# First loads, one product, eight squares and one addition moved in a cross-attention and FFN kernel

## The chip, the core and the metric

The kernel runs on one core of one Trainium2 chip. The core has five engines, each with an instruction queue of its own that is worked off in order: TensorE (PE, matrix products; PEld is its weight load), VectorE (DVE), ScalarE (ACT), GpSimd (POOL) and SyncE (SP, which here only issues DMAs). Engines wait for each other through semaphores. The metric is the device time of one launch in microseconds (us), the median of several runs; lower is better.

## The reference

There are 128 sequences of 64 rows with 128 features. `_prob` is a shifted tanh divided by its row sum. Cut to what is computed:

```python
def xattn(q, k, v, ...):                      # q = layernorm(x), k = v = ctx
    q_prob, k_prob = _prob(q), _prob(k)
    log_ratio = jnp.log(q_prob) - jnp.log(k_prob)
    sid = jnp.einsum('bnd,bmd->bnm', q_prob - k_prob, log_ratio)
    attn = jax.nn.softmax(-sid / D ** 0.5, axis=-1)
    f_diff = (v - attn @ v) @ W_diff.T + b_diff + q
    h = _layernorm(f_diff, ln_g, ln_b)
    mlp = gelu(h @ W1.T + b1) @ W2.T + b2     # 128 -> 512 -> 128
    return _layernorm(mlp + f_diff, ln_g, ln_b)

x = x + xattn(layernorm(x), ctx, ctx, ...)
x = x + fp8_linear(layernorm(x), weight) + bias
```

## The kernel before

The 8192 rows are 64 tiles of 128 rows. Four tiles are a chunk (16 chunks); in stages two and three the last chunk is cut into two halves, which makes 17 pieces (NA = NP = 17), numbered from 0. Every stage is a software pipeline: `run_steps` calls a step function per engine, in which `at(lag)` is the piece that entered `lag` steps ago. The order on each engine is the order in which the step function is written.

**Stage one** (`phase1`, to 62.9 us). Per chunk SP loads ctx and x into two buffers each: the load of ctx chunk k waits until ACT has taken the tanh of chunk k-2 (`tanh_k`) and PE has turned it, that of x until DVE has the variance of chunk k-2 (`x_var`). PE transposes ctx (L1058) and multiplies it by W_diff (L1067), then adds the row b_diff with a selection matmul (L1076). ACT takes tanh of ctx (L556), copies the transposed ctx (L561) and the product (L567), and takes tanh of normalised x (L572). DVE computes the statistics of x (L835 to L798), normalises x into F (L867) and adds the product to F (L840). POOL raises the variance to the power -0.5 (L376) and adds the row ln_b to X (`add_to_x`, L368) for the final residual. The rows b_diff and ln_b come in by two DMAs (L546, L547) that ACT's queue issues; DVE centres b_diff and splits it in two parts (L750 to L764) ahead of its first chunk.

**Stage two** (`phase2`, to about 122 us). Per piece: ACT takes Ln (L617), Exp of the scores (L627), copies two transposed operands out of PSUM (L642 and L644, called dT and lT), and makes half of the k parts of the difference (L607). DVE finishes the difference (L904) and the log ratio (L916), and adds the attention product to F (L939). POOL does the k parts of two tiles (L389) and the whole of one tile (L395, L409, L400, L414). PE transposes difference and log ratio (L1166, L1172), forms the scores (L1154) and the attention product (L1139). In the last steps the MLP of the first two pieces is prepared: ACT squares F with a sum (L599, `squares`, four tiles each), takes Ln and Exp of the variance (L653, L656), DVE scales F into h (L878, `take_h`), PE turns h (L1099, `turn_h`), ACT and DVE split it in a high part (L588, `upper_half`) and a low part (L883, `lower_half`), and PE begins the first matmuls (L1109 to L1111, `mlp1`). Before the first gelu (L594) ACT loads another function table (L630).

**Stage three** (`phase3`). The MLP, the second norm, both residuals and the quantised linear layer, with the same kind of pipeline. Variances of pieces 2 on come from `squares` on ACT and `norm_power` on POOL (L507, L509), in pairs of pieces. POOL also issues DMAs that add bias rows to F (L441, L497), and between the stages quantises the weight of the last layer (L457 to L469).

The functions that the change touches, with the lines of the profile:

## Time and profile before

| | us |
|---|---|
| median of 3 runs | 255.77 (255.61 to 256.09) |
| the profiled execution's own time | 255.62 |
| its span, first to last instruction | 253.7 |
| TensorE's mean granted clock | 0.958 of full speed |

| engine | busy us | share of the span | instructions |
|---|---|---|---|
| PE | 210.8 | 83% | 1777 |
| DVE | 221.2 | 87% | 842 |
| ACT | 216.9 | 86% | 781 |
| POOL | 190.6 | 75% | 255 |

A busy share is an average over three stages with different limits, so each stage is read by itself: which engine never waits there, and who is waited for. Instructions of one engine overlap a little in the record (the next one starts some 0.1 us before the last one's end is written), so spacings are taken from start to start. The profiled execution's time is 1.92 us more than its span, and 0.15 us under the median.

### The profile page before, as it was taken

The page shows a single profiled execution, that of the slowest core. Times are in us where ns is not written, and L with a number is a line of the kernel's source. Part 1 is how long each engine was busy: PE and PEld are TensorE (multiplying, and loading weights), DVE is VectorE, ACT ScalarE, POOL GpSimd, SP SyncE. Part 2 cuts the span into 40 slices and gives each one's busy share as a digit, 9 for nine tenths or more (in the row PEclk, how much of TensorE's full clock was granted, in tenths as well). Part 3 has the DMA queues.
Part 4 walks back from the last instruction along what each step waited for, and adds up shares of the span by engine and source line. Part 5 has one row for each costly group of instructions (what it writes and reads, how often), then busy time and mean ns, then how long its engine had stood idle before and what let it go on. Part 6 is the DMA issues. An engine that isn't in the chain of part 4 may idle for free.

```text
span 253.7 us, 6046 instructions
## 1 busy us (share of the span) xinstructions
PE 210.8 (83%) x1777; PEld 181.4 (71%) x1777; DVE 221.2 (87%) x842; ACT 216.9 (86%) x781; POOL 190.6 (75%) x255
## 2 busy tenths in 40 slices
PE   2686685987499888877899999999999999998721
PEld 1666463876386666656699999988998999887610
DVE  1899999998899999999525889999999999999983
ACT  4599999998999999979997889998888777876673
...
GB/s 136 191 191 199 162 153 164 162 115 16 3 3 0 3 3 1 3 1 3 44 25 93 18 98 145 98 148 111 145 128 120 131 144 119 127 129 115 97 43 124
DMA packets 50817, 23.52 MB, mean 93 GB/s; under 512 B 9313, under 2 KB 50657, under 8 KB 50785
## 3 DMA queue, kind: packets, MB, share of 16 engines
...
q10 hardware_dynamic: 432, 0.20, 0.3%
q14 instruction: 19, 0.15, 0.2%
...
## 4 chain that ended last, share of the span: by engine, by line
POOL 30%; DVE 24%; issue 11%; PE 6%; ACT 4%; DVEq 0%; POOLq 0%; ACTq 0%
POOL F L441 6%; POOL xrstd L483 5%; POOL orstd L476 4%; POOL F L497 4%; DVE q_c L904 3%; DVE F L939 3%; PE bank L1118 3%; POOL q_c L389 3%; DVE LN_c L916 3%; DVE F L962 3%; DVE xstat L973 2%; DVE LN_c L982 2%; POOL LN_c L409 2%; DVE F L967 2%; POOL E_c L395 2%
## 5 line engine op out<-in xcount | busy, mean ns | idle before, releaser
L1118 PEld LDWEIGHTS bank<-W2T,TQK 128*128 128x128 f32 x512 | 62.9, 191 | 4.6 <-ACT TQK L594 1.3
L1118 PE MATMUL bank<-W2T,TQK 128*128 128x128 f32 x512 | 64.5, 277 | 1.1 <-ACT TQK L594 1.1
L594 ACT ACTIVATE TQK<-bank,b1c 128x512 f32<-128x512 f32 (+1 forms) x68 | 42.9, 662 | 5.6 <-PE bank L1111 5.0
L483 POOL TENSOR_TENSOR xrstd<-xvar,pow_c 128x4 f32<-128x4 f32 (+1 forms) x17 | 18.6, 1093 | 20.1 <-DVE xvar L798 20.1
L376 POOL TENSOR_TENSOR xrstd<-xvar,pow_c 128x4 f32<-128x4 f32 x16 | 16.8, 1052 | 22.0 <-DVE xvar L798 22.0
L1109 PE MATMUL bank<-hTh,W1h 128*128 128x512 f32 (+1 forms) x68 | 30.0, 442 | 0.8 <-DVE hTl L883 0.8
L441 POOL DMA_DIRECT2D F<-rows x17 | 26.0, 1529 | 5.8 <-DVE E_c L878 5.8
L1110 PE MATMUL bank<-hTl,W1h 128*128 128x512 f32 (+1 forms) x68 | 26.0, 382 | 0.0
L1111 PE MATMUL bank<-hTh,W1l 128*128 128x512 f32 (+1 forms) x68 | 25.8, 380 | 0.0
L1067 PE MATMUL bank<-WdT,vT_c 128*128 128x128 f32 x128 | 21.3, 318 | 3.4 <-ACT vT_c L561 2.6
L1067 PEld LDWEIGHTS bank<-WdT,vT_c 128*128 128x128 f32 x128 | 18.8, 226 | 5.7 <-ACT vT_c L561 5.7
L1058 PE MATMUL bank<-ident,LN_c 128*128 128x128 f32 x64 | 12.6, 330 | 11.0 <-DMA LN_c<-in_ctx_dram 10.9
L556 ACT ACTIVATE TQK<-LN_c 128x128 f32<-128x128 f32 x64 | 19.4, 335 | 1.9 <-DMA LN_c<-in_ctx_dram 1.9
L497 POOL DMA_DIRECT2D F<-rows x14 | 18.6, 1326 | 3.2 <-issue 2.7
L368 POOL TENSOR_TENSOR X<-X,rows 128x512 f32<-128x512 f32 x16 | 20.4, 1272 | 0.4 <-DVE F L867 0.3
L572 ACT ACTIVATE TQK<-F 128x128 f32<-128x128 f32 x64 | 19.6, 347 | 0.7 <-DVE F L867 0.7
L678 ACT ACTIVATE TQK<-F 128x128 f32<-128x128 f32 x64 | 19.0, 313 | 0.7 <-DVE F L957 0.7
L904 DVE SCALAR_TENSOR_TENSOR q_c<-TQK,GAINQ,q_c 128x128 f32<-128x128 f32 x49 | 19.6, 450 | 0.0
L1139 PE MATMUL bank<-PV,E_c 64*64 64x129 f32 x256 | 18.3, 281 | 1.4 <-ACT E_c L627 1.4
L711 ACT ACTIVATE LN_c<-LN_c 128x512 bf16<-128x512 fp8e4 x13 | 8.2, 631 | 13.1 <-DVE LN_c L982 13.1
L1058 PEld LDWEIGHTS bank<-ident,LN_c 128*128 128x128 f32 x64 | 8.8, 168 | 14.5 <-DMA LN_c<-in_ctx_dram 14.2
L599 ACT ACTIVATE TQK<-F 128x128 f32<-128x128 f32 x64 | 19.0, 311 | 0.0
...
## 6 DMA issues: line engine op xcount, KB each, us to landing
...
```

What stands on the lines that cost most here:

```text
L368: pool.tensor_tensor(tiles(chunk(X, k)), tiles(chunk(X, k)), over_tiles(b_r, k.g), ALU.add).then_inc(xb_ready, 1)
L441: pool.dma_start(tiles(chunk(F, k)), over_tiles(b2_r, k.g), accum_op=ALU.add).then_inc(b2_added[k.n % 3], 16)
L483: pool.tensor_tensor(buf(xrstd, x1, G), buf(xvar, x1, G), pow_c[:, 0:x1.g], ALU.pow).then_inc(x1_rstd, 1)
L497: pool.dma_start(tiles(chunk(F, x1)), over_tiles(bf_r, x1.g), accum_op=ALU.add).then_inc(bf_added[x1.n % 3], 16)
L594: act.activation(hid(m, j), m1_bank(m, j), ACT.Gelu, bias=b1c[:, j:j + 1]).then_inc(gelu_ready, 1)
L904: last = dve.scalar_tensor_tensor(out=tile(diff_c, k, i), in0=all_tile(TQ, k, i), scalar=per_tile(GAINQ, k, i), in1=tile(diff_c, k, i), op ...
L1058: last = pe.transpose(VT_B[k.buf][:, i * D:(i + 1) * D], tile(ctx_c, k, i), ident[:, :])
L1067: last = pe.matmul(P_B[k.n % 3][:, i * D:(i + 1) * D], tile(vT_c, k, i), WdT[:, :], start=(i == 0), stop=False, skip_group_check=True)
L1109: pe.matmul(ps, w_hi, buf(hTh, m), start=True, stop=False)
L1110: pe.matmul(ps, w_hi, buf(hTl, m), start=False, stop=False)
L1111: pe.matmul(ps, w_lo, buf(hTh, m), start=False, stop=True).then_inc(m1_ps, 1)
L1118: last = pe.matmul(M2_B[m.buf][:, i * D:(i + 1) * D], hid(m, j)[:, i * D:(i + 1) * D], W2T[:, j * D:(j + 1) * D], start=(j == 0 and i == 0 ...
```

## The change

1. SP issues the loads of ctx and x for chunks 0 and 1, then the two rows b_diff and ln_b, then goes on. ACT issues only W_diff.
2. DVE centres and splits b_diff after the normalisation of chunk 0, and no longer ahead of the first statistics.
3. PE multiplies chunk 0 by W_diff before it transposes chunk 1, and ACT copies this product between the tanh of chunk 1 and the copy of the transposed chunk 1.
4. The squares of pieces 0 and 1 are no longer two runs of four in steps 15 and 16 of stage two. Each of the steps 7 to 14 has one, between the copies dT and lT. Ln and Exp follow for both pieces together in step 15.
5. `take_h`, `turn_h`, `upper_half` and `lower_half` of piece 0 each come one step earlier.
6. POOL's addition of ln_b to the last chunk of X leaves step 15 of stage two and comes after `norm_power` of piece 3.

```diff
@@ -91,2 +91,3 @@
     EARLY = 2
+    SQUARES_AT = 6
     NORM_CUTS = (0, 4, 8, NC)
@@ -319,3 +320,7 @@
 
-            for k in chunks[0:5]:
+            for k in chunks[0:2]:
+                load(k)
+            sp.dma_start(bd_r, b_diff.unsqueeze(0).broadcast_to([P, D])).then_inc(bd_in, 16)
+            sp.dma_start(b_r, ln_b.unsqueeze(0).broadcast_to([P, D])).then_inc(br_in, 16)
+            for k in chunks[2:5]:
                 load(k)
@@ -432,4 +437,2 @@
                         log_ratio(k, G - 1)
-                if is_piece(k, NA - 2):
-                    add_to_x(chunks[NC - 1])
 
@@ -527,2 +530,3 @@
             norm_power(pieces[3])
+            add_to_x(chunks[NC - 1])
             run_steps(pieces, 1, phase3)
@@ -545,4 +549,2 @@
             act.dma_start(Wd_raw, W_diff).then_inc(wd_in, 16)
-            act.dma_start(bd_r, b_diff.unsqueeze(0).broadcast_to([P, D])).then_inc(bd_in, 16)
-            act.dma_start(b_r, ln_b.unsqueeze(0).broadcast_to([P, D])).then_inc(br_in, 16)
             act.wait_ge(wd_ps, 1)
@@ -550,2 +552,8 @@
 
+            def keep_product(k):
+                act.wait_ge(P_ps, k.n + 1)
+                if is_piece(k, 0):
+                    act.wait_ge(consts, CONSTS)
+                act.activation(pv_chunk(k), tiles(P_B[k.n % 3][:, 0:k.g * D]), ACT.Copy).then_inc(P_sb, 1)
+
             def phase1(at):
@@ -558,2 +566,4 @@
                     last.then_inc(tanh_k, 1)
+                    if is_piece(k, 1):
+                        keep_product(chunks[0])
                     act.wait_ge(vT_ps, k.n + 1)
@@ -562,7 +572,4 @@
                 k = at(1)
-                if k.live:
-                    act.wait_ge(P_ps, k.n + 1)
-                    if is_piece(k, 0):
-                        act.wait_ge(consts, CONSTS)
-                    act.activation(pv_chunk(k), tiles(P_B[k.n % 3][:, 0:k.g * D]), ACT.Copy).then_inc(P_sb, 1)
+                if k.live and k.n > 0:
+                    keep_product(k)
                 k = at(2)
@@ -595,2 +602,6 @@
 
+            def square(k, i):
+                return act.activation(all_tile(TK, k, i), all_tile(F, k, i), ACT.Square,
+                                      scale=float(D) ** -0.5, accum_out=per_tile(VARF, k, i))
+
             def squares(k):
@@ -598,4 +609,3 @@
                 for i in range(k.g):
-                    last = act.activation(all_tile(TK, k, i), all_tile(F, k, i), ACT.Square,
-                                          scale=float(D) ** -0.5, accum_out=per_tile(VARF, k, i))
+                    last = square(k, i)
                 last.then_inc(fvar_ready, 1)
@@ -642,2 +652,9 @@
                     act.activation(buf(dT_c, k), D_B[:, 0:k.g * D], ACT.Copy).then_inc(dT_sb, 1)
+                    nth = k.n - SQUARES_AT
+                    if 0 <= nth < EARLY * G:
+                        first = pieces[nth // G]
+                        act.wait_ge(f_half, (first.at + first.g) // 2)
+                        last = square(first, nth % G)
+                        if nth % G == G - 1:
+                            last.then_inc(fvar_ready, 1)
                     act.wait_ge(lT_ps, k.n + 1)
@@ -647,13 +664,11 @@
                     kparts(k)
-                k = at(0)
-                if k.n >= NA - 2 and k.live:
-                    first = pieces[k.n - (NA - 2)]
-                    squares(first)
-                    act.wait_ge(fvar_ready, first.n + 1)
-                    act.activation(of_tiles(VARF, first), of_tiles(VARF, first), ACT.Ln,
+                if is_piece(at(1), SQUARES_AT + EARLY * G):
+                    act.wait_ge(fvar_ready, EARLY)
+                    act.activation(VARF[:, 0:EARLY * G], VARF[:, 0:EARLY * G], ACT.Ln,
                                    bias=eps_c[:, 0:1]).then_inc(fln_ready, 1)
-                    act.wait_ge(fln_ready, first.n + 1)
-                    act.activation(of_tiles(RSTDF, first), of_tiles(VARF, first), ACT.Exp,
-                                   scale=-0.5).then_inc(frstd, 1)
-                if is_piece(at(2), NA - 2):
+                    act.wait_ge(fln_ready, 1)
+                    for first in pieces[0:EARLY]:
+                        act.activation(of_tiles(RSTDF, first), of_tiles(VARF, first), ACT.Exp,
+                                       scale=-0.5).then_inc(frstd, 1)
+                if is_piece(at(2), NA - 3):
                     upper_half(pieces[0])
@@ -771,6 +786,2 @@
             dve.tensor_copy(sel[:, :], sel_raw).then_inc(sel_ready, 1)
-            dve.wait_ge(bd_in, 16)
-            centre_row(bd_r, 0).then_inc(bd_ready, 1)
-            dve.wait_ge(bd_ready, 1)
-            split_row(bd_r, bd_hl[:, :], 0).then_inc(bd_hl_ready, 1)
 
@@ -869,2 +880,7 @@
                     last.then_inc(q_ready, 1)
+                if is_piece(q, 0):
+                    dve.wait_ge(bd_in, 16)
+                    centre_row(bd_r, 0).then_inc(bd_ready, 1)
+                    dve.wait_ge(bd_ready, 1)
+                    split_row(bd_r, bd_hl[:, :], 0).then_inc(bd_hl_ready, 1)
 
@@ -926,8 +942,7 @@
                     centre_row(b2_r, 2).then_inc(rows_ready, 1)
-                if is_piece(k, NA - 1):
+                if is_piece(k, NA - 2):
                     dve.wait_ge(frstd, 1)
+                    dve.wait_ge(diff_pool, NC - 1)
                     take_h(pieces[0])
                 k = at(2)
-                if is_piece(k, NA - 2):
-                    lower_half(pieces[0])
                 if k.live:
@@ -943,2 +958,4 @@
                             last.then_inc(f_half, 1)
+                if is_piece(k, NA - 3):
+                    lower_half(pieces[0])
                 if is_piece(k, NA - 2):
@@ -959,2 +976,4 @@
             def residual(x1):
+                if is_piece(x1, NC - 1):
+                    dve.wait_ge(xb_ready, NC)
                 dve.wait_ge(orstd_ready, x1.n + 1)
@@ -1021,3 +1040,3 @@
 
-            dve.wait_ge(xb_ready, NC)
+            dve.wait_ge(xb_ready, NC - 1)
             run_steps(pieces, 1, phase3)
@@ -1046,2 +1065,10 @@
 
+            def products(k):
+                pe.wait_ge(vT_sb, k.n + 1)
+                wait(pe, pq_ready, k.n - 2)
+                for i in range(k.g):
+                    last = pe.matmul(P_B[k.n % 3][:, i * D:(i + 1) * D], tile(vT_c, k, i), WdT[:, :],
+                                     start=(i == 0), stop=False, skip_group_check=True)
+                last.then_inc(P_ps, 1)
+
             def phase1(at):
@@ -1052,2 +1079,5 @@
                     keep_busy(10)
+                if is_piece(at(1), 0):
+                    pe.wait_ge(wd_sb, 1)
+                    products(at(1))
                 k = at(0)
@@ -1059,12 +1089,4 @@
                     last.then_inc(vT_ps, 1)
-                k = at(1)
-                if k.live:
-                    if is_piece(k, 0):
-                        pe.wait_ge(wd_sb, 1)
-                    pe.wait_ge(vT_sb, k.n + 1)
-                    wait(pe, pq_ready, k.n - 2)
-                    for i in range(k.g):
-                        last = pe.matmul(P_B[k.n % 3][:, i * D:(i + 1) * D], tile(vT_c, k, i), WdT[:, :],
-                                         start=(i == 0), stop=False, skip_group_check=True)
-                    last.then_inc(P_ps, 1)
+                if at(1).live and at(1).n > 0:
+                    products(at(1))
                 k = at(2)
@@ -1125,3 +1147,3 @@
                 k = at(2)
-                if is_piece(k, NA - 2):
+                if is_piece(k, NA - 3):
                     turn_h(pieces[0])
```

In the following rows the line numbers of the kernel after the change differ from those of before; the operands tell which is which.

DVE, from its first statistics to the statistics of chunk 2. Before, with the five instructions on b_diff (`rows`, `row_mean`, `bd_hl`) in front:

```order
L750 TENSOR_REDUCE row_mean<-rows 128x1
L752 TENSOR_SCALAR row_mean<-row_mean 128x1
L754 TENSOR_SCALAR rows<-rows,row_mean 128x128
L761 CAST bd_hl<-rows 128x128
L764 TENSOR_TENSOR bd_hl<-rows,bd_hl 64x128
L835 BN_STATS xstat<-X 128x6 x4
```

After, the end of the normalisation of chunk 0 (F) and what stands behind it:

```order
L878 TENSOR_SCALAR F<-X,xmv,xrstd 128x128 x4
L765 TENSOR_REDUCE row_mean<-rows 128x1
L767 TENSOR_SCALAR row_mean<-row_mean 128x1
L769 TENSOR_SCALAR rows<-rows,row_mean 128x128
L776 CAST bd_hl<-rows 128x128
L779 TENSOR_TENSOR bd_hl<-rows,bd_hl 64x128
L846 BN_STATS xstat<-X 128x6 x4
```

The five instructions have moved from in front of everything to between chunk 0's F and chunk 2's statistics.

ACT, steps 15 and 16 of stage two, from the copy dT (`vT_c<-bank`) of piece 14 to the table load. Before (NRATIO holds the variances, HALFK their inverse roots):

```order
L642 ACTIVATE vT_c<-bank 128x512
L644 ACTIVATE lT_c<-bank 128x512
L607 ACTIVATE q_c<-TQK,SHIFT,GAINK 128x128
L599 ACTIVATE TQK,NRATIO<-F 128x128 x4
L653 ACTIVATE NRATIO<-NRATIO,eps_c 128x4
L656 ACTIVATE HALFK<-NRATIO 128x4
L617 ACTIVATE LN_c<-TQK,half_c 128x2x256
L627 ACTIVATE E_c<-bank 128x256
L642 ACTIVATE vT_c<-bank 128x256
L644 ACTIVATE lT_c<-bank 128x256
L599 ACTIVATE TQK,NRATIO<-F 128x128 x4
```

After:

```order
L652 ACTIVATE vT_c<-bank 128x512
L661 ACTIVATE lT_c<-bank 128x512
L617 ACTIVATE q_c<-TQK,SHIFT,GAINK 128x128
L667 ACTIVATE NRATIO<-NRATIO,eps_c 128x8
L671 ACTIVATE HALFK<-NRATIO 128x4 x2
L627 ACTIVATE LN_c<-TQK,half_c 128x2x256
L637 ACTIVATE E_c<-bank 128x256
L652 ACTIVATE vT_c<-bank 128x256
L661 ACTIVATE lT_c<-bank 128x256
L595 ACTIVATE hTh<-bank 128x512
```

Both runs of four squares are gone from here, and the upper half of piece 0 follows in the same step.

POOL, from the weight's last product to the first bias DMAs of stage three. Before:

```order
L469 TENSOR_TENSOR NORM<-NORM,RNORM 128x128
L507 TENSOR_TENSOR NRATIO<-NRATIO,eps_c 128x8
L509 TENSOR_TENSOR HALFK<-NRATIO,pow_c 128x8
L441 DMA F<-rows 128x4x128
L507 TENSOR_TENSOR NRATIO<-NRATIO,eps_c 128x8
```

After:

```order
L472 TENSOR_TENSOR NORM<-NORM,RNORM 128x128
L510 TENSOR_TENSOR NRATIO<-NRATIO,eps_c 128x8
L512 TENSOR_TENSOR HALFK<-NRATIO,pow_c 128x8
L373 TENSOR_TENSOR X<-X,rows 128x512
L444 DMA F<-rows 128x4x128
```

The addition to X now stands directly behind the power for which DVE's `take_h` of piece 2 waits.

## Rows read from the trace of the kernel before

**Rows 1.** Windows: stretch, length, busy us (and instructions) of each engine, clock, DMA.
```profile
20.00:40.00 20.00, 14.23 (x93) 12.05 (x94) 19.30 (x96) 20.00 (x111) 13.64 (x12) 0.91 0.59 169
...
80.00:100.00 20.00, 17.77 (x244) 13.89 (x244) 20.00 (x76) 19.50 (x39) 19.41 (x37) 1.00 0.01 2
...
160.00:200.00 40.00, 40.00 (x291) 36.47 (x290) 37.73 (x129) 36.17 (x132) 32.67 (x33) 1.00 0.91 129
```
**Rows 2.** Timeline, first 13 us: start, duration, engine, line, count, [idle before, releaser].
```profile
5.89 0.29 DVE L750 TENSOR_REDUCE row_mean<-rows 128x1 f32<-128x128 f32 x1 [4.17 <-DMA rows<-in_L_xattn_b_diff_dram]
...
6.98 0.29 DVE L764 TENSOR_TENSOR bd_hl<-rows,bd_hl 64x128 fp32r<-64x128 f32 x1
7.65 0.87 DVE L835 BATCH_NORM_STATS2 xstat<-X 128x6 f32<-128x128 f32 x4 [0.38 <-DMA X<-in_x_dram]
...
8.57 0.31 ACT L556 ACTIVATE TQK<-LN_c 128x128 f32<-128x128 f32 x1 [1.89 <-DMA LN_c<-in_ctx_dram]
...
11.45 0.60 ACT L567 ACTIVATE PV<-bank 128x512 f32<-128x512 f32 x1 [1.11 <-PE bank L1067]
...
12.19 1.26 POOL L368 TENSOR_TENSOR X<-X,rows 128x512 f32<-128x512 f32 x1
...
12.36 0.87 DVE L835 BATCH_NORM_STATS2 xstat<-X 128x6 f32<-128x128 f32 x4 [0.33 <-DMA X<-in_x_dram]
```
**Rows 3.** Timeline of DVE, 21 to 29 us.
```profile
21.68 0.87 DVE L835 BATCH_NORM_STATS2 xstat<-X 128x6 f32<-128x128 f32 x4 [0.17 <-DMA X<-in_x_dram]
...
28.02 0.87 DVE L835 BATCH_NORM_STATS2 xstat<-X 128x6 f32<-128x128 f32 x4
28.99 0.69 DVE L840 TENSOR_TENSOR F<-bank,F 128x512 f32<-128x512 f32 x1
```
**Rows 4.** Timeline, end of stage one.
```profile
59.40 1.27 POOL L368 TENSOR_TENSOR X<-X,rows 128x512 f32<-128x512 f32 x1
59.90 0.86 DVE L867 TENSOR_SCALAR F<-X,xmv,xrstd 128x128 f32<-128x128 f32 x1
...
61.56 0.31 ACT L572 ACTIVATE TQK<-F 128x128 f32<-128x128 f32 x1 [0.65 <-DVE F L867]
```
**Rows 5.** Timeline, one step in the middle of stage two.
```profile
95.04 1.14 ACT L617 ACTIVATE LN_c<-TQK,half_c 128x1024 f32<-128x1024 f32 x1
...
96.34 0.59 ACT L642 ACTIVATE vT_c<-bank 128x512 f32<-128x512 f32 x1
96.82 0.60 POOL L409 TENSOR_SCALAR LN_c<-LN_c,LRATIO 128x128 f32<-128x128 f32 x1
...
97.02 0.60 ACT L644 ACTIVATE lT_c<-bank 128x512 f32<-128x512 f32 x1
```
**Rows 6.** Timeline, last steps of stage two.
```profile
111.78 1.29 POOL L368 TENSOR_TENSOR X<-X,rows 128x512 f32<-128x512 f32 x1
...
111.87 1.35 DVE L916 SCALAR_TENSOR_TENSOR LN_c<-LN_c,LRATIO 128x128 f32<-128x128 f32 x1
...
115.11 0.30 ACT L599 ACTIVATE TQK<-F 128x128 f32<-128x128 f32 x1
...
115.40 0.29 ACT L599 ACTIVATE TQK<-F 128x128 f32<-128x128 f32 x1
...
117.88 1.10 PE L1139 MATMUL bank<-PV,E_c 64*64 64x129 f32 x16 [1.45 <-ACT E_c L627]
...
121.70 1.28 ACT L630 ACT_TABLE_LOAD   x1
...
122.16 0.47 PE L1109 MATMUL bank<-hTh,W1h 128*128 128x512 f32 x1 [0.80 <-DVE hTl L883]
```
**Rows 7.** Timeline, start of stage three.
```profile
130.08 1.38 POOL L441 DMA_DIRECT2D F<-rows  x1
...
130.20 0.69 DVE L878 TENSOR_TENSOR E_c<-F,HALFK 128x512 f32<-128x512 f32 x1 [3.14 <-POOL HALFK L509]
...
131.21 0.60 PE L1099 MATMUL bank<-ident,E_c 128*128 128x128 f32 x4
```

## The prediction

> **What bounds the kernel now.** I read the windows first, because the shares over the whole span mix three stages. In stage one ACT is busy all the time and DVE 19.30 of 20 us; in stage two DVE is busy all the time, with ACT (19.50) and POOL (19.41) close behind; in stage three PE is busy 40.00 of 40 us [rows 1]. So three things count: when DVE finishes stage one, how long the steps of stage two are, and when PE can begin the MLP. Then I read the timeline at both borders. At the end of stage one ACT is the one that waits: its last tanh stands 0.65 us idle for DVE's F [rows 4]. So DVE, not ACT, ends stage one, although ACT has the fuller row. From 122.16 us PE runs without a pause that matters; what it waits for there (0.80 us) is the lower half of piece 0 [rows 6]. A shift of that point reaches the end, unless PE is stopped later.
>
> **The first loads.** The two rows on ACT's queue are 64 KB each and share the 16 DMA engines with the first four chunk loads. DVE's first statistics begin at 7.65, behind 0.38 us of waiting for x, and ACT's second tanh at 8.57, behind 1.89 us of waiting for ctx [rows 2]. Up to 7.65 about 1.1 MB have come in, of which the rows are 0.13; in proportion they cost (0.13/1.1) x (7.65 - 2) = 0.6 us. The engines aren't full in this stretch, so less can come of it: I take 0.4, from 0.2 to 0.6. SP issues the rows two places ahead of the load of ctx chunk 2, which waits for the first tanh in any case, so they delay nothing. ACT gains more than the 0.4: the product of chunk 0 is no longer behind the transposes of chunk 1, so most of the 1.11 us ahead of the copy at 11.45 goes too [rows 2]. ACT will be about 1.1 us early. I book none of it, since ACT waits for DVE at the end of the stage anyway.
>
> **The five DVE instructions on b_diff.** They run from 5.89 to 7.27, 1.38 us [rows 2]. Before, all but nothing of this cost time, as x landed only later. Now they stand between F of chunk 0 and the statistics of chunk 2, on the engine that ends the stage. DVE waited 0.33 us until 12.36 for x, so it was free at 12.03, or 11.95 with the usual overlap; with 0.4 us gained that is 11.55, and with some 1.3 us added start to start the statistics of chunk 2 begin at 12.9 instead of 12.36: +0.5. DVE then loses waits that it has now. The wait for x of 0.17 at 21.68 goes, with 0.1 in front of it, and three times (as at 28.99, where L840 starts 0.10 after the end of the statistics in front) L840 waits 0.1 to 0.2 us for ACT's tanh, which now comes earlier [rows 3]. That is 0.7 in all. So alone, moving them costs 0.5 - 0.7 = -0.2 us: nothing.
> But they get a neighbour. POOL starts the addition to X (L368, 1.26 us) 0.15 us after F of chunk 0 [rows 2], that is at 11.8 to 13.05, just beside them. At the end of the stage a DVE instruction of the same form as the third of them (tensor_scalar, 128x128) that begins while L368 runs takes 0.86 us and ends 0.09 after L368 does [rows 4]; three of four such instructions in the same group take about 0.34. By this row the third instruction, due at 12.1, ends at 13.2 instead of 12.3, and the fourth and fifth follow: +0.85. Stage one then ends 0.65 us later than before. Range: -0.2 (no collision) to +0.8. I take 0.65, since the form is the same.
>
> **The squares in the steps of stage two.** A square with its sum takes 0.29 us from start to start (115.11 to 115.40) [rows 6]. In a step ACT's copy dT begins at 96.34 and the next, lT, at 97.02; dT lasts 0.59, and its neighbours of that size follow each other after 0.5. So 0.1 to 0.18 us per step is spare and the square adds 0.1 to 0.2 to each of eight steps: ACT falls behind by 0.8 (up to 1.6) at the end. What hides this is distance: Ln begun at 95.04 ends at 96.18, and POOL uses it at 96.82, 0.64 us later [rows 5]; DVE uses it only some 2.4 us later, and the k parts 2.1 us later. Until the seventh square ACT is 0.7 behind. I book 0.1 us; the range is 0 to 0.9. Where the cover is gone, POOL and soon DVE move by what is over.
>
> **The last steps of stage two.** Three terms, not to be added, since they lie beside each other; I followed the chain with the durations of the trace.
> First, L368 at 111.78 goes. Beside it one L916 took 1.35 us instead of about 0.3 [rows 6]: -1.0 on DVE, and PE's transposes of log ratio, ACT's lT and all behind them follow.
> Second, ACT has no squares (4 x 0.29 = 1.2 us, with Ln and Exp 1.7) ahead of Ln of piece 16 and Exp of piece 14. PE waited 1.45 us for that Exp, until 117.88 [rows 6]. Now: lT of piece 14 at 113.3, the shared Ln and two Exps to 114.8, Ln of piece 16 to 115.4, Exp to 115.8, and PE at 116.1. That is -1.8.
> Third, the chain of h. `take_h` of piece 0 runs at 114.7 to 115.4, so the upper half is ready at 116.9. The lower half then waits only for its turn on DVE, behind F of piece 14: 118.95 to 119.6. PE begins the MLP at 119.65 instead of 122.16: -2.5. On ACT the last Exp follows at 119.25, the table load (1.28 us, before at 121.70 [rows 6]) at 119.5, and gelu can begin at 120.8, 2.2 us earlier than the load ends now (122.98). So PE is 2.5 and ACT 2.2 us early, less what stages one and two give away.
> POOL reaches the weight's quantisation some 3 us earlier and has it done before it is wanted.
>
> **The moved addition on POOL.** Only about one microsecond of POOL's time is shifted here, and POOL waits again later. The neighbour is the question again. Before, behind the power (L509) POOL issues a DMA at 130.08, and DVE, released by the same power, starts `take_h` of piece 2 at 130.20; PE turns it at 131.21 [rows 7], 0.32 us after it ends at 130.89. Now L368 stands in the DMA's place and begins 0.1 us ahead of `take_h`, which reads two SBUF operands as L916 did. L916, begun 0.09 after L368, ended 0.15 after it [rows 6]. Its 128 columns fit into that; `take_h` has 512, about 0.55 us of work, so it would end near 130.08 + 1.27 + 0.55 = 131.9, 1.0 late. PE has 0.3 us to spare. At this point the gain is then 2.2 + 0.3 - 1.0 = 1.5 us instead of 2.5. If `take_h` wins, POOL waits and the gain is 2.5. I take 1.5: POOL was first by about as much in the row.
> The Trainium skill ("SBUF — State Buffer", section Who interferes with whom) says that a DVE instruction with two SBUF inputs and a GpSimd one that reads SBUF exclude each other, and whichever starts first holds the ports for all of its instruction. By this rule both collisions happen, unless DVE is first at `take_h`; the rows on L916 and L867 agree with it.
>
> **Sum**, against the profiled execution: +0.65 (stage one) + 0.1 (steps) - 1.5 (border of stage three) = -0.75 us. It measured 255.62, 0.15 under the median of the runs shown; set against that median of 255.77 I get 255.0 us.
>
> **The rivals.**
> A. One collision only. Without that on b_diff: -0.2 + 0.1 - 1.5 = -1.6; without that on `take_h`: 0.65 + 0.1 - 2.5 = -1.75. About 254.1. For it speaks that 0.1 us decides who is first; against it that POOL came first in both rows.
> B. No collision: -0.2 + 0.1 - 2.5 = -2.6, 253.2. It needs both 0.1 us to fall the other way.
> C. ACT becomes the bound of stage two, and the kernel gets slower. If a lone square costs ACT its 0.30 and the read of its sum 0.19 one after the other instead of 0.29, each step is over by 0.3 to 0.4, 8 steps by 2.4 to 3.1; less the 0.64 of cover that leaves about 2.1, of which I take 2.0 as late at the border. Then +0.65 + 2.0 - 1.5 = +1.15, 256.9. It decides from 0.24 us over per step ((0.75 + 0.64 + 0.5)/8). Against it: four squares in a row, and a copy behind such a tanh, all follow after 0.29.
> D. The change doesn't do what it says: the gain is kept by something else at the border, for instance rows b_diff that ACT's earlier tanh doesn't need and a `lower_half` that still waits. Then only stage one counts, and the time is 255.6 to 256.2.
>
> **How the numbers follow.** Forecast 0.47, A 0.30, B 0.09, C 0.07, D 0.07. The forecast's own terms give 255.0 within 0.5. The range takes in the forecast, A and the better part of D, and leaves out C and most of B: 253.5 to 255.9. A measurement of this kernel can tell about 0.2%, 0.5 us, from no change. Faster by more than that, under 255.26: two thirds of the forecast (0.32), A and B, 0.71. Within it: the rest of the forecast and most of D, 0.20. Slower: C and a rest of D, 0.09.
>
> **What the profile would show.** Right: the last tanh of stage one waits longer than 0.65 us for DVE; the third of the b_diff instructions lasts near 1 us; the steps of stage two stay at 3.25 us; in step 14 no L916 over 0.5 us; PE's first MLP matmul 1.7 to 2.0 us earlier than 122.16; `take_h` of piece 2 lasts over 1.2 us, and PE stops behind it. Wrong: steps with squares longer than 3.3 us, POOL waiting for Ln in them, a first MLP matmul at 122 or later, or a stage one that ends earlier than before.

## The result, and the profile after

| | before | after |
|---|---|---|
| median of 4 runs each, side by side | 255.69 (255.22 to 256.09) | 253.16 (252.62 to 253.33) |
| the profiled execution's own time | 255.62 | 252.62 |
| its span | 253.7 | 250.7 |

The ratio of the runs is 0.9892, 95% interval 0.9871 to 0.9912: 2.5 us faster by the medians, 2.8 by the ratio, and faster by more than the forecast, whose range ended at 253.5. A second set of runs of the changed kernel gave the same ratio (0.9892, 0.9872 to 0.9911). Two executions of the experiments below were in a slower state (403.61 and 501.79 us) and count in no ratio.

The rows of the changed kernel that answer to those of before, group by group. Line numbers have moved: L846 is DVE's statistics, L878 its normalisation, L373 POOL's addition to X, L604 ACT's square, L1131 the first MLP matmul.

Windows, as [rows 1] (columns: stretch, length, busy us and instructions of PE, PEld, DVE, ACT, POOL, clock, DMA share, GB/s):

```profile
20.00:40.00 20.00, 15.05 (x100) 12.40 (x100) 19.60 (x98) 20.00 (x111) 13.77 (x12) 0.93 0.59 164
80.00:100.00 20.00, 17.93 (x252) 13.90 (x248) 20.00 (x74) 20.00 (x49) 19.41 (x39) 1.00 0.01 2
160.00:200.00 40.00, 40.00 (x291) 36.34 (x291) 37.95 (x125) 34.89 (x123) 32.40 (x35) 1.00 0.88 129
```

In stage two ACT has become as full as DVE (20.00 of 20 us, 19.50 before); the rest stands as it was.

Timeline of the first 13 us, as [rows 2]:

```profile
5.21 0.87 DVE L846 BATCH_NORM_STATS2 xstat<-X 128x6 f32<-128x128 f32 x4 [3.48 <-DMA X<-in_x_dram]
...
6.22 0.30 ACT L564 ACTIVATE TQK<-LN_c 128x128 f32<-128x128 f32 x1
...
8.55 0.60 ACT L557 ACTIVATE PV<-bank 128x512 f32<-128x512 f32 x1 [1.06 <-PE bank L1070]
...
9.81 1.27 POOL L373 TENSOR_TENSOR X<-X,rows 128x512 f32<-128x512 f32 x1
...
10.08 1.08 DVE L769 TENSOR_SCALAR rows<-rows,row_mean 128x128 f32<-128x128 f32 x1
...
11.79 0.87 DVE L846 BATCH_NORM_STATS2 xstat<-X 128x6 f32<-128x128 f32 x4
```

Here lies the surprise. The first statistics begin 2.44 us earlier (5.21, not 7.65), ACT's second tanh 2.35 us earlier (6.22, not 8.57). The forecast had 0.4. Then DVE does the five instructions on b_diff, of which the third (L769) takes 1.08 us beside POOL's addition, as forecast, and the statistics of chunk 2 begin at 11.79, still 0.57 earlier than before.

End of stage one, as [rows 4]:

```profile
58.60 1.69 DVE L878 TENSOR_SCALAR F<-X,xmv,xrstd 128x128 f32<-128x128 f32 x4
...
60.33 0.31 ACT L579 ACTIVATE TQK<-F 128x128 f32<-128x128 f32 x1 [0.89 <-DVE F L878]
```

The last tanh waits 0.89 us for DVE (0.65 before) and begins 1.23 us earlier (61.56 before); forecast was 0.65 later.

One step of stage two, as [rows 5]:

```profile
94.11 1.18 ACT L627 ACTIVATE LN_c<-TQK,half_c 128x1024 f32<-128x1024 f32 x1
...
95.41 0.63 ACT L652 ACTIVATE vT_c<-bank 128x512 f32<-128x512 f32 x1
...
95.89 0.35 ACT L604 ACTIVATE TQK<-F 128x128 f32<-128x128 f32 x1
...
96.18 0.64 ACT L661 ACTIVATE lT_c<-bank 128x512 f32<-128x512 f32 x1
...
97.43 1.19 ACT L627 ACTIVATE LN_c<-TQK,half_c 128x1024 f32<-128x1024 f32 x1
```

The square (L604) stands between the copies dT and lT; they start 0.77 us apart instead of 0.68, and the step lasts 3.32 us instead of 3.25.

The last steps, as [rows 6], and the start of stage three, as [rows 7]:

```profile
110.43 0.92 DVE L932 SCALAR_TENSOR_TENSOR LN_c<-LN_c,LRATIO 128x128 f32<-128x128 f32 x3
...
114.88 1.10 PE L1161 MATMUL bank<-PV,E_c 64*64 64x129 f32 x16
...
118.40 1.28 ACT L640 ACT_TABLE_LOAD   x1
...
118.65 0.47 PE L1131 MATMUL bank<-hTh,W1h 128*128 128x512 f32 x1 [0.59 <-DVE hTl L899]
```
```profile
124.66 0.20 POOL L510 TENSOR_TENSOR NRATIO<-NRATIO,eps_c 128x8 f32<-128x8 f32 x1 [1.71 <-ACT TQK L604]
...
126.59 1.29 POOL L373 TENSOR_TENSOR X<-X,rows 128x512 f32<-128x512 f32 x1
126.70 1.73 DVE L894 TENSOR_TENSOR E_c<-F,HALFK 128x512 f32<-128x512 f32 x1 [3.14 <-POOL HALFK L512]
...
128.49 0.66 PE L1121 MATMUL bank<-ident,E_c 128*128 128x128 f32 x4 [0.62 <-DVE E_c L894]
```

DVE's three log ratios of that step take 0.92 us together, and none meets the addition. PE's attention product behind the freed Exp begins at 114.88 instead of 117.88: 3.00 earlier, of which 1.23 come from stage one and 1.77 from here (forecast 1.8). The MLP begins at 118.65 (122.16 before). POOL's addition at 126.59 is 0.11 us ahead of the scaling of piece 2, which takes 1.73 us instead of 0.69, and PE waits 0.62 us for it.

Measured from the last tanh of stage one, so that the stages come apart (single executions, start to start):

| | before | after | difference | forecast |
|---|---|---|---|---|
| last tanh of stage one begins | 61.56 | 60.33 | -1.23 | +0.65 |
| from there to the first MLP matmul | 60.60 | 58.32 | -2.28 | -2.4 |
| from there to PE's turn of piece 2 | 69.65 | 68.16 | -1.49 | -1.4 |
| from that turn to the end of the span | 122.49 | 122.21 | -0.28 | 0 |

So the second half of the forecast held in this execution almost to the tenth (some of that is luck, as the spread of these stretches shows further down), and the first half failed. The experiments ask what made the first loads so much faster, and what each part of the change is worth.

### The profile page after: what moved, and what is told of

It is laid out like the page before. It is cut to its first block, busy times and chain, and to the rows that moved or that the text cites. A ratio compares the mean times of both kernels' runs of the same rounds, so it can differ in the third digit from the quotient of the medians.

```text
span 250.7 us, 6047 instructions
## 1 busy us (share of the span) xinstructions
PE 212.1 (85%) x1777; PEld 181.2 (72%) x1777; DVE 221.9 (89%) x842; ACT 216.3 (86%) x780; POOL 191.1 (76%) x255
## 4 chain that ended last, share of the span: by engine, by line
POOL 29%; ACT 14%; DVE 14%; issue 13%; PE 5%; DVEq 0%; ACTq 0%; POOLq 0%
POOL F L444 8%; POOL xrstd L486 7%; POOL orstd L479 5%; POOL F L500 5%; ACT LN_c L627 3%; ACT q_c L617 3%; DVE LN_c L932 2%; DVE q_c L920 2%; POOL HALFK L512 2%; DVE F L954 2%; ACT lT_c L661 1%; ACT E_c L637 1%; PE bank L1140 1%; ACT vT_c L652 1%; DVE F L981 1%
## 5 line engine op out<-in xcount | busy, mean ns | idle before, releaser
L1131 PE MATMUL bank<-hTh,W1h 128*128 128x512 f32 (+1 forms) x68 | 30.0, 442 | 0.6 <-DVE hTl L899 0.6
L373 POOL TENSOR_TENSOR X<-X,rows 128x512 f32<-128x512 f32 x16 | 20.3, 1271 | 0.2 <-DVE F L878 0.2
L579 ACT ACTIVATE TQK<-F 128x128 f32<-128x128 f32 x64 | 19.7, 354 | 0.9 <-DVE F L878 0.9
L693 ACT ACTIVATE TQK<-F 128x128 f32<-128x128 f32 x64 | 19.0, 313 | 1.0 <-DVE F L974 1.0
L604 ACT ACTIVATE TQK<-F 128x128 f32<-128x128 f32 x64 | 19.5, 319 | 0.0
L627 ACT ACTIVATE LN_c<-TQK,half_c 128x1024 f32<-128x1024 f32 (+1 forms) x17 | 19.0, 1118 | 0.0
L726 ACT ACTIVATE LN_c<-LN_c 128x512 bf16<-128x512 fp8e4 x13 | 8.2, 632 | 12.1 <-DVE LN_c L1001 12.1
L479 POOL TENSOR_TENSOR orstd<-ovar,pow_c 128x4 f32<-128x4 f32 (+1 forms) x17 | 17.3, 1016 | 1.3
L1001 DVE TENSOR_SCALAR LN_c<-F,xmv,xrstd 128x128 fp8e4<-128x128 f32 x56 | 15.6, 343 | 2.9 <-POOL xrstd L486 2.7
```

The lines of the kernel that those rows point to most:

```text
L479: pool.tensor_tensor(buf(orstd, k, G), buf(ovar, k, G), pow_c[:, 0:k.g], ALU.pow).then_inc(orstd_ready, 1)
L627: act.activation(ln_both(k), tanh_both(k), ACT.Ln, bias=half_c[:, 0:1], scale=TANH_GAIN).then_inc(ln_ready, 1)
L1131: pe.matmul(ps, w_hi, buf(hTh, m), start=True, stop=False)
```

## The experiments

All ratios are to the kernel before, run on the same chip beside the kernel in question; where two of them are compared, their difference times 255.7 us is the price, good to 0.6 to 0.8 us by the intervals. The two kernels compared did not always run on the same chip, which the ratios can only take out as far as it touches both alike. "Stage one" stands for DVE's and ACT's new order and the rows' new place together.

### What stretched the first loads

**Theory B**: a load that copies one row of HBM to 128 partitions reads the same 512 B 128 times, is slow for its 64 KB, and beside the chunk loads on a second queue holds them up. **Rivals**: any transfer on a second queue does that (Q); only the bytes count (M); or the gain at the start came from the new order (O).

**Rows back on ACT's queue, all else changed.**

```diff
-            sp.dma_start(bd_r, b_diff.unsqueeze(0).broadcast_to([P, D])).then_inc(bd_in, 16)
-            sp.dma_start(b_r, ln_b.unsqueeze(0).broadcast_to([P, D])).then_inc(br_in, 16)
...
             act.dma_start(Wd_raw, W_diff).then_inc(wd_in, 16)
+            act.dma_start(bd_r, b_diff.unsqueeze(0).broadcast_to([P, D])).then_inc(bd_in, 16)
+            act.dma_start(b_r, ln_b.unsqueeze(0).broadcast_to([P, D])).then_inc(br_in, 16)
```

> The changed kernel with one thing put back: the two row loads (b_diff, ln_b) are issued by ACT's queue right behind W_diff, as before the change. Everything else stays changed. Theory S (the row loads stretched the loads of the first chunks from beside them, and taking them away gave about 2.2 us of the gain): x of chunk 0 lands as late as before, DVE's first statistics at about 7.6 us and not 5.2, chunk 2's statistics about 12.6 to 13.0, time 255.0 to 255.6. Rival O (the gain at the start came from the new order of work on PE, ACT and DVE, and the early landing only filled it): first statistics at 7.6 but chunk 2's at 11.8 to 12.1, time 253.2 to 253.8.

Measured 255.28 us, ratio 0.9983 (0.9965 to 1.0001). Its timeline:

```profile
7.47 0.87 DVE L846 BATCH_NORM_STATS2 xstat<-X 128x6 f32<-128x128 f32 x4 [5.75 <-DMA X<-in_x_dram]
```
```profile
62.46 0.31 ACT L579 ACTIVATE TQK<-F 128x128 f32<-128x128 f32 x1 [0.89 <-DVE F L878]
```

x of chunk 0 is late again by 2.26 us (7.47 against 5.21), and stage one ends 2.13 us later than in the changed kernel (62.46 against 60.33). Nearly all of the shift at the start reaches the end of the stage. By the ratios the loads' place is worth 2.3 us: O has fallen. My figure for the statistics of chunk 2 (12.6 to 13.0) missed: they begin at 14.02, 2.23 us later than in the changed kernel.

**Two more loads on ACT's queue: dense, and broadcast.** Both kernels are the changed one with one pair of loads added, into free space of `lT_c`.

```diff
             act.dma_start(Wd_raw, W_diff).then_inc(wd_in, 16)
+            act.dma_start(lT_c[:, C + 0*D:C + 1*D], W_diff).then_inc(extra_in, 16)
+            act.dma_start(lT_c[:, C + 1*D:C + 2*D], W_diff).then_inc(extra_in, 16)
```
```diff
             act.dma_start(Wd_raw, W_diff).then_inc(wd_in, 16)
+            act.dma_start(lT_c[:, C + 0*D:C + 1*D], b_diff.unsqueeze(0).broadcast_to([P, D])).then_inc(extra_in, 16)
+            act.dma_start(lT_c[:, C + 1*D:C + 2*D], ln_b.unsqueeze(0).broadcast_to([P, D])).then_inc(extra_in, 16)
```

> The changed kernel, and ACT issues two more loads of 64 KB behind its own W_diff, each of the whole matrix W_diff into free space (128 rows of 512 B that lie behind one another in HBM). Theory B (what stretches the first chunk loads is that a row load reads the same 512 B 128 times): these do not, x of chunk 0 lands 0.2 to 0.5 us later than in the changed kernel (their bytes, 0.13 MB at some 300 GB/s, are 0.4 us), time 253.2 to 253.7. Rival Q (any transfer of a second queue takes its share beside SP's): first statistics near 7.6 us and time 255.0 to 255.6, as with the row loads on ACT.

> The changed kernel, and ACT issues two more row loads (b_diff and ln_b again, broadcast to 128 partitions, 64 KB each) behind W_diff, into free space; nobody waits for them before stage two. Theories B and Q both say first statistics at 7.3 to 7.9 us and time 255.0 to 255.9; the bytes alone (theory M) say 5.6 us and 253.2 to 253.7.

Measured: dense 252.98 us, ratio 0.9897 (0.9869 to 0.9924), no different from the changed kernel; broadcast 256.27 us, ratio 1.0019 (1.0002 to 1.0036), 3.2 us more than the changed kernel by the ratios and 3.1 more than the dense pair. The same queue, size and place; only the source differs. The dense pair cost even less than theory B had booked for its bytes: x of chunk 0 came 0.10 us later (5.31 against 5.21) where 0.2 to 0.5 were expected, and the time is 0.2 under the expected range. The DMA view of the first 9 us of the one with dense loads (columns: what, issuing engine, count, size, median us from issue to landing):

```profile
X<-in_x_dram SPq DMA_DIRECT2D x3, 256.0 KB, 4.0
lT_c<-in_L_xattn_W_diff_dram ACTq DMA_DIRECT2D x2, 64.0 KB, 3.5
```

and of the one with broadcast loads:

```profile
LN_c<-in_ctx_dram SPq DMA_DIRECT2D x3, 256.0 KB, 5.4
X<-in_x_dram SPq DMA_DIRECT2D x3, 256.0 KB, 5.6
...
lT_c<-in_L_xattn_b_diff_dram ACTq DMA_DIRECT2D x1, 64.0 KB, 4.4
lT_c<-in_L_xattn_ln_b_dram ACTq DMA_DIRECT2D x1, 64.0 KB, 6.1
rows<-in_L_xattn_b_diff_dram SPq DMA_DIRECT2D x1, 64.0 KB, 7.7
```

Two dense loads land 3.5 us after their issue and leave x at 4.0 (3.9 in the changed kernel); two broadcast ones take 4.4 and 6.1, and x takes 5.6. The windows of 3 to 6 us (the DMA share is added up from the times of the packets and can come out above 1) say what the DMA engines do meanwhile, with the dense pair and then with the broadcast pair:

```profile
3.00:4.00 1.00, 0.56 (x2) 0.50 (x2) 0.00 (x0) 0.43 (x1) 0.00 (x0) 1.00 1.12 335
4.00:5.00 1.00, 1.00 (x5) 0.72 (x4) 0.00 (x0) 0.75 (x5) 0.00 (x0) 1.00 1.15 310
5.00:6.00 1.00, 0.32 (x2) 0.00 (x0) 0.69 (x4) 1.00 (x7) 0.00 (x0) 1.00 1.20 296
```
```profile
3.00:4.00 1.00, 0.45 (x2) 0.48 (x2) 0.00 (x0) 0.45 (x1) 0.00 (x0) 1.00 0.78 225
4.00:5.00 1.00, 1.00 (x6) 0.73 (x5) 0.00 (x0) 0.65 (x4) 0.00 (x0) 1.00 0.51 146
5.00:6.00 1.00, 0.29 (x2) 0.00 (x0) 0.00 (x0) 1.00 (x7) 0.00 (x0) 1.00 0.89 258
```

With dense loads beside them the chunks come in at some 300 GB/s, with broadcast loads at 225, 146 and 258, and the DMA engines show as busy for only 0.51 of the time at the lowest point, though three loads of 256 KB are still to come in (ctx of chunk 0 landed at 4.1 us). The kernel before and the changed one show the same pair of pictures (before first):

```profile
3.00:4.00 1.00, 0.04 (x1) 0.07 (x1) 0.00 (x0) 0.43 (x1) 0.00 (x0) 1.00 0.68 196
4.00:5.00 1.00, 1.00 (x4) 0.83 (x5) 0.00 (x0) 0.24 (x2) 0.00 (x0) 1.00 0.52 136
```
```profile
3.00:4.00 1.00, 0.40 (x2) 0.43 (x2) 0.00 (x0) 0.00 (x0) 0.00 (x0) 1.00 1.12 336
4.00:5.00 1.00, 0.99 (x5) 0.69 (x5) 0.00 (x0) 0.60 (x4) 0.00 (x0) 1.00 1.03 281
```

Theory B stands, Q and M have fallen. The Trainium skill ("DMA: Bandwidth & Descriptors", section Rules for kernel authors) says that loads issued by different engines run on the same 16 DMA engines and interleave, so that a second queue gives no bandwidth; the dense pair agrees (335, 310 and 296 GB/s in the three windows, 336, 281 and 289 without it), and the page says nothing of what a broadcast source costs. Two of my numbers for the broadcast pair missed: x came at 6.83 and not at 7.3 to 7.9, and the time was 0.4 above my range. The second x chunk was delayed still more (its statistics began at 9.93; 6.94 in the changed kernel, 9.19 with the two rows back on ACT's queue). These 0.74 us over the kernel with the rows back are there again at the last tanh (63.20 against 62.46). SP's own queue was held too: its issue of the row b_diff took 1.72 us, 0.58 in the changed kernel. Why such a load stalls the others while the engines show as half idle isn't settled.

**The rows with SP, but the old order.** The kernel before with the loads' move alone.

```diff
-            act.dma_start(bd_r, b_diff.unsqueeze(0).broadcast_to([P, D])).then_inc(bd_in, 16)
-            act.dma_start(b_r, ln_b.unsqueeze(0).broadcast_to([P, D])).then_inc(br_in, 16)
...
-            for k in chunks[0:5]:
+            for k in chunks[0:2]:
+                load(k)
+            sp.dma_start(bd_r, b_diff.unsqueeze(0).broadcast_to([P, D])).then_inc(bd_in, 16)
+            sp.dma_start(b_r, ln_b.unsqueeze(0).broadcast_to([P, D])).then_inc(br_in, 16)
+            for k in chunks[2:5]:
                 load(k)
```

> The kernel before with one thing changed: SP and not ACT issues the two row loads, behind the loads of chunks 0 and 1. DVE still centres b_diff ahead of its first statistics. Theory S: x of chunk 0 has landed by 5.2 us, but DVE now waits for the row until about 8.1 us and its five instructions end at about 9.5, so its first statistics begin at about 9.6 (7.65 before): the loads alone cost 1 to 2 us, 256.7 to 257.7. If the time is under 255.7, DVE's place behind the row was no loss and the loads' move is worth its gain alone.

Measured 256.59 us, ratio 1.0028 (1.0007 to 1.0050): 0.7 us slower than before, just under what I expected. DVE waits for b_diff until 7.66 us (I had 8.1) and begins its statistics at 9.07. So each half of the change in stage one, by itself, makes the kernel slower: the loads alone +0.7, and the new order alone +1.5 (next section). Together they gain 0.8. The loads bring x in early, and the new order lets DVE use it.

### What each half of the change is worth

**The border alone**: stage one and its loads as before, everything else as changed.

```diff
-            sp.dma_start(bd_r, b_diff.unsqueeze(0).broadcast_to([P, D])).then_inc(bd_in, 16)
-            sp.dma_start(b_r, ln_b.unsqueeze(0).broadcast_to([P, D])).then_inc(br_in, 16)
...
+            act.dma_start(bd_r, b_diff.unsqueeze(0).broadcast_to([P, D])).then_inc(bd_in, 16)
+            act.dma_start(b_r, ln_b.unsqueeze(0).broadcast_to([P, D])).then_inc(br_in, 16)
...
+            dve.wait_ge(bd_in, 16)
+            centre_row(bd_r, 0).then_inc(bd_ready, 1)
+            dve.wait_ge(bd_ready, 1)
+            split_row(bd_r, bd_hl[:, :], 0).then_inc(bd_hl_ready, 1)
...
-                if is_piece(q, 0):
-                    dve.wait_ge(bd_in, 16)
-                    centre_row(bd_r, 0).then_inc(bd_ready, 1)
-                    dve.wait_ge(bd_ready, 1)
-                    split_row(bd_r, bd_hl[:, :], 0).then_inc(bd_hl_ready, 1)
```

(and the product of chunk 0 back in its old place on PE and ACT).

> The kernel with the second half of the change alone: squares of pieces 0 and 1 in the steps, the MLP work of piece 0 one step earlier, POOL's last addition in stage three. Loads, b_diff on DVE and the first product are as before. Theory of the prediction (the border is worth 1.5 us, the steps with squares cost 0.1): last tanh of stage one at 61.6 us as before, first MLP matmul near 119.8 (122.16 before), piece 2's turn near 129.8 (131.2), time 253.9 to 254.5. Rival E (the steps with squares cost nothing and the border's whole 2.4 us stay): 253.0 to 253.5. Rival N (the gain of the whole change is all at the start): 255.3 to 255.9.

Measured 253.89 us, ratio 0.9923 (0.9907 to 0.9938).

```profile
61.17 0.31 ACT L577 ACTIVATE TQK<-F 128x128 f32<-128x128 f32 x1 [0.77 <-DVE F L880]
```
```profile
119.49 0.47 PE L1127 MATMUL bank<-hTh,W1h 128*128 128x512 f32 x1 [0.58 <-DVE hTl L896]
...
127.54 1.72 DVE L891 TENSOR_TENSOR E_c<-F,HALFK 128x512 f32<-128x512 f32 x1 [3.14 <-POOL HALFK L510]
```

From the last tanh to the MLP it is 58.32 us, the very figure of the changed kernel (by luck, given the spread below), and the scaling of piece 2 takes its 1.72 us. The time lies at the fast edge of the theory's range: -2.0 us by the ratio, where the forecast had -1.4 for steps and border together. The trace accounts for -1.5 up to the turn of piece 2 and -0.3 behind it. It also shows how far a single execution can be trusted: stage one is the same code as before and ends 0.39 us earlier.

The parts, from the ratios:

| part | from, to | price in us | forecast |
|---|---|---|---|
| squares, steps and border | before, border alone | -2.0 | -1.4 |
| new order of stage one, rows on ACT's queue | border alone, rows back on ACT's queue | +1.5 | +1.05 |
| rows to SP's queue | rows back on ACT's queue, changed kernel | -2.3 | -0.4 |
| all | before, changed kernel | -2.8 | -0.75 |

**The last addition back in stage two.**

```diff
+                if is_piece(k, NA - 2):
+                    add_to_x(chunks[NC - 1])
...
             norm_power(pieces[3])
-            add_to_x(chunks[NC - 1])
```

> The changed kernel with one thing put back: POOL adds ln_b to the last chunk of X in step 15 of stage two again, and not behind the power of piece 3. Theory: the log ratio or another DVE instruction of the last steps meets it and loses 0.6 to 0.8 us there, while the scaling of piece 2 takes 0.69 us and not 1.73, so piece 2's turn comes at about the same time: within 0.3 us of the changed kernel, 252.8 to 253.4. Rival W (the addition's old place was worth the whole border): 254.0 to 254.7.

Measured 252.94 us, ratio 0.9880 (0.9861 to 0.9899): no different from the changed kernel, as the theory says. The scaling of piece 2 takes 0.69 us again, but the MLP begins 59.47 us after the last tanh instead of 58.32, and the turn of piece 2 comes at 68.52 us instead of 68.16. So moving the addition gained nothing that can be told in sum, which fits what the theory says: what it frees in stage two it takes back in stage three. In stage two the addition (113.12, 1.27 us) meets two of DVE's differences (L921), which take 0.86 us together and 0.60 in the changed kernel: 0.26 us, where I had 0.6 to 0.8. The rest of the 1.15 us can't be put down to it, since that stretch varies by a microsecond by itself (more on this below).

### The two collisions

**The addition one place earlier**, in POOL's 1.71 us of waiting ahead of 124.66.

```diff
-            norm_power(pieces[3])
             add_to_x(chunks[NC - 1])
+            norm_power(pieces[3])
```

> The changed kernel with POOL's last addition one place earlier: ahead of the power of piece 3 and not behind it, into the 1.7 us in which POOL waits for ACT's squares. Theory P (the scaling of piece 2 takes 1.73 us because it meets the addition): it takes 0.69 us, piece 2's turn comes 0.7 to 1.0 us earlier, and the time falls by 0.4 to 0.9 us to 252.2 to 252.7. Rival: stage three is bound by PE and ACT and the start of piece 2 is made good within it, so that 0 to 0.2 us are left (252.8 to 253.1).

Measured 252.51 us, ratio 0.9870 (0.9850 to 0.9889).

```profile
123.60 1.28 POOL L373 TENSOR_TENSOR X<-X,rows 128x512 f32<-128x512 f32 x1
...
127.39 0.69 DVE L894 TENSOR_TENSOR E_c<-F,HALFK 128x512 f32<-128x512 f32 x1 [3.14 <-POOL HALFK L512]
...
128.40 0.60 PE L1121 MATMUL bank<-ident,E_c 128*128 128x128 f32 x4
```

The collision is gone: the same scaling takes 0.69 us with the addition out of its way, 1.73 beside it. By the ratios that is worth 0.6 us, within what the theory said, though the intervals overlap; the same edit made once more below gives 0.6 again. In this execution the MLP began at 119.34, 0.69 us later than in the changed kernel's, in a stretch that the edit doesn't touch, which hides the gain in the timeline's own times.

**POOL's first addition held back** until b_diff is split.

```diff
                     if is_piece(k, 0):
                         pool.wait_ge(br_in, 16)
+                        pool.wait_ge(bd_hl_ready, 1)
```

> The changed kernel with POOL's first addition to X held until DVE has split b_diff (a wait on POOL). Theory P: DVE's subtraction of the row's mean takes 0.29 us and not 1.08, so the statistics of chunk 2 begin about 0.8 us earlier (11.0 us), unless they meet the addition in turn; 0.5 to 0.8 us of it reach the end of stage one, time 252.2 to 252.7. Rival: the collision only moves to the statistics or the next normalisation and nothing is won: 252.8 to 253.3.

Measured 252.88 us, ratio 0.9889 (0.9867 to 0.9911): nothing won.

```profile
9.98 0.29 DVE L770 TENSOR_SCALAR rows<-rows,row_mean 128x128 f32<-128x128 f32 x1
...
10.89 0.87 DVE L847 BATCH_NORM_STATS2 xstat<-X 128x6 f32<-128x128 f32 x4
...
11.00 1.27 POOL L373 TENSOR_TENSOR X<-X,rows 128x512 f32<-128x512 f32 x1 [1.33 <-DVE bd_hl L780]
...
11.87 0.42 DVE L795 TENSOR_TENSOR xmv<-xstat 128x8 f32<-128x8 f32 x1
```

The subtraction of the mean takes 0.29 us and not 1.08, and the statistics of chunk 2 begin 0.90 us earlier than in the changed kernel. But now the addition meets the small instructions behind the statistics (L795 takes 0.42 us, 0.17 in the changed kernel), and of the 0.90 us 0.65 are left at the statistics of chunk 3 (13.85 against 14.50) and 0.29 at the last tanh (60.04 against 60.33). The rival was right: the collision only moved.

### A version that beats both

The selection matmul uses only partitions 0 and 64 of b_diff (its selection matrix is zero elsewhere). So two loads of 512 B can take the place of 128 reads, early enough for DVE to do its five instructions while x is still on its way.

```diff
             act.dma_start(Wd_raw, W_diff).then_inc(wd_in, 16)
+            act.wait_ge(bd_zero, 1)
+            act.dma_start(bd_r[0:1, :], b_diff.unsqueeze(0)).then_inc(bd_in, 16)
+            act.dma_start(bd_r[S:S + 1, :], b_diff.unsqueeze(0)).then_inc(bd_in, 16)
...
-            sp.dma_start(bd_r, b_diff.unsqueeze(0).broadcast_to([P, D])).then_inc(bd_in, 16)
...
+            dve.memset(bd_r, 0.0).then_inc(bd_zero, 1)
...
+            dve.wait_ge(bd_in, 32)
+            centre_row(bd_r, 0).then_inc(bd_ready, 1)
+            dve.wait_ge(bd_ready, 1)
+            split_row(bd_r, bd_hl[:, :], 0).then_inc(bd_hl_ready, 1)
```

> The changed kernel, but b_diff is loaded into partitions 0 and 64 only (two loads of 512 B by ACT's queue behind W_diff, into a row block that DVE has set to zero), which is all that the selection matmul reads, and DVE centres and splits it ahead of its first statistics again. The row load of ln_b stays with SP. Theory B (the 128 reads of one row are what is slow): two reads disturb nothing, x of chunk 0 lands as in the changed kernel, DVE's five instructions end by 5.5 us, and the 2.2 us between the normalisation of chunk 0 and the statistics of chunk 2 (9.58 to 11.79) fall to a wait for x of chunk 2, which lands near 10.8: 0.8 to 1.2 us faster than the changed kernel, 251.8 to 252.3. Rival Q2 (any small load ahead of or beside the chunk loads delays them): first statistics after 6.5 us, no gain, 252.8 to 253.6.

Measured 252.21 us, ratio 0.9859 (0.9842 to 0.9876); the changed kernel, run beside it:

> The changed kernel as it is, for comparison on the same chip with the three that follow. 252.6 to 253.3 us.

gave 253.30 us, ratio 0.9892 (0.9872 to 0.9911). So 1.1 us by the medians, 0.8 by the ratios, as expected.

```profile
4.38 0.29 DVE L767 TENSOR_REDUCE row_mean<-rows 128x1 f32<-128x128 f32 x1 [2.38 <-DMA rows<-in_L_xattn_b_diff_dram]
...
5.79 0.87 DVE L853 BATCH_NORM_STATS2 xstat<-X 128x6 f32<-128x128 f32 x4
...
10.28 0.87 DVE L853 BATCH_NORM_STATS2 xstat<-X 128x6 f32<-128x128 f32 x4 [0.17 <-DMA X<-in_x_dram]
```

DVE has b_diff at 4.38, its first statistics start 0.6 us later than in the changed kernel and those of chunk 2 1.5 us earlier (10.28 against 11.79). This is theory B once more: the small loads on ACT's queue, of the same row, do not hold up x of chunk 0 (3.9 us from issue to landing, as in the changed kernel).

The run of the changed kernel beside it has a warning in its trace. The profiled execution (254.53 us, the longest of six) began as the first one did (statistics of chunk 2 at 11.93, 11.79 there), yet

```profile
61.48 0.31 ACT L579 ACTIVATE TQK<-F 128x128 f32<-128x128 f32 x1 [0.25 <-DVE F L878]
```

its last tanh is 1.15 us later. Between 27 and 56 us five of its eight steps were 0.14 to 0.28 us longer. Stage one varies by a microsecond from one execution to the next, and the stretch from the last tanh to the first MLP matmul by as much: 58.32 us in the first execution of the changed kernel, 59.04 in this one, 58.2 to 59.5 over eleven of kernels with the changed border. Differences of that size need the medians beside the trace.

In stage one the trace shows where some of it comes from. TensorE's granted clock stood at its lower level (0.50 of full speed, 1.2 GHz) from about 29.1 to 36 us here and only from about 43.1 to 46.6 in the first execution. Just before it fell PE did little in both (no instruction on record from 28 to 29 us here, 0.17 us of work from 42 to 43 there), and while it was low PE was busy throughout (5.99 us of the 6 from 30 to 36). ACT waited for PE three times between 30 and 38 us, 1.3 us in sum, and in the first execution it waited for nothing between 26 and 57 us. So a few more microseconds at the lower clock put PE in front of ACT even in this stage; that they account for the whole 1.15 us isn't shown.

**With the addition ahead of the power as well** (the same edit as above).

> As the kernel with two rows, and POOL's last addition ahead of the power of piece 3. The two gains add: 251.2 to 251.8 us (0.5 us under the kernel with two rows alone). If the collision in stage three is worth nothing, 251.8 to 252.3.

Measured 251.69 us, ratio 0.9836 (0.9816 to 0.9855): 0.5 us under the one before it by the medians, 0.6 by the ratios. The gains add.

**And x one chunk ahead.**

```diff
-        x_in = [sem(f"x_in{i}") for i in range(2)]
+        x_in = [sem(f"x_in{i}") for i in range(3)]
...
                 wait(sp, x_var, k.n - 1)
-                sp.dma_start(tiles(chunk(X, k)), x_d[:, k.at:k.at + k.g]).then_inc(x_in[k.buf], 16)
+                if k.n < 2:
+                    load_x(k)
+                if 0 < k.n < NC - 1:
+                    load_x(chunks[k.n + 1])
```

> As the last, and SP issues each x chunk one chunk earlier (x has room for all chunks; a third semaphore lets three loads be under way), so x of chunk 2 goes out right behind that of chunk 1, with ctx as before. If DVE waits for x of chunk 2 in the kernel with two rows, that wait (about 1.0 us) goes: statistics of chunk 2 near 9.6 us, 250.2 to 251.2. Rival: the extra 256 KB in the first 5 us delay ctx of chunk 2 or the first x, or ACT becomes what bounds the first chunks, and the time stays within 0.3 us of the kernel before it.

Measured 251.46 us, ratio 0.9830 (0.9811 to 0.9849). Against the kernel without it nothing that can be told (0.2 us, as the rival had it); my 250.2 to 251.2 was wrong. The wait that I meant to remove was small to begin with: the kernel with two rows waits 0.17 us for x at 10.28, since DVE is busy with chunks 0 and 1 until then. By the ratios the two fastest kernels are 1.4 and 1.6 us under the changed one, 4.2 and 4.3 under the one before.

## Why the prediction was wrong, point by point

- **What bounds the kernel**: right. DVE ends stage one (the last tanh waits 0.89 us for it), and a shift of the MLP's start reaches the end: the turn of piece 2 came 2.72 us earlier, the span ended 3.0 us earlier.
- **The first loads**: this step failed. I took the rows' share of the bytes, (0.13/1.1) x 5.65 us (I wrote 0.6; it is 0.67, and 0.6 with the 1.2 MB that the view gives up to 7.65 us), lowered it to 0.4 because "the engines aren't full in this stretch", and kept 0.2 to 0.6 as its range. Measured are 2.44 us at DVE's first statistics (2.26 with the rows' place alone put back) and 2.3 us of time. The bytes were the wrong measure, since the same 0.13 MB from a dense source cost nothing that could be measured. And the engines' half-idle state, with three or four large loads waiting, was read the wrong way round: it was no reason to expect less, but the sign that something other than bytes held the loads up. The range should have been bounded from above by a full rate: the changed kernel has 281 to 336 GB/s where the one before had 136 and 196. One of the prediction's own signs of being wrong showed with it, a stage one that ends earlier than before.
- **The five instructions on b_diff**: right. The collision took place (1.08 us, forecast 1.1: from 12.1 to 13.2), and the order alone costs 1.5 us by the ratios, 1.29 in the traces (62.46 against 61.17), where the forecast without the 0.4 was 1.05.
- **The squares in the steps**: right. DVE's k part at 109.10 (110.22 before) is 1.12 us earlier, of 1.23 at the end of stage one: 0.1 lost, as booked. ACT is over by 0.07 us per step, a little under the 0.1 to 0.2 that I gave it; my line for "wrong", steps over 3.3 us, was set too tight, since 3.32 did no harm.
- **The last steps**: right, -2.28 at the first MLP matmul for a forecast of -2.5 and +0.1, though with a stretch that varies by a microsecond the close match is partly luck. The ratios give -2.0 for steps and border together; -1.4 was somewhat too little.
- **The moved addition**: right in mechanism, and near in size. The scaling took 1.73 us where 1.7 had been worked out (130.2 to 131.9), and without the collision the time is 0.6 us less, where 1.0 was booked. The rule of the Trainium skill ("SBUF — State Buffer", section Who interferes with whom) held at `take_h`, which reads two SBUF operands: the one that started first kept its pace (1.29 us, 1.28 when alone), the other waited. The same happened to the third b_diff instruction (POOL 1.27 us, DVE 1.08 instead of 0.29). But that one reads a single tile besides one value per partition, so the rule on two inputs, as the prediction gives it, doesn't speak of it. The same section has another clause for `tensor_scalar`, that it can take both of DVE's port pairs, and this time agrees with that; in the forecast the row on L867, an instruction of the same form, carried the price.
- **The sum**: its frame held, and the one term that sank it is that for the first loads, 0.4 for 2.3 us, wrong in its mechanism (a share of the bytes) and so in its size. With 2.3 it would have been 0.65 - 1.9 + 0.1 - 1.5 = -2.65, 253.1 us. That this lies so close to the 2.8 and 2.5 us measured is partly luck: by the ratios the new order cost 0.45 more than booked and the border gave 0.6 more, which all but cancel. Rival B stood at about that time (253.2), with no collision; both collisions took place, so it was right in its number and wrong in its reason.
